# S4 convolution and LSTM-like scan on one core: the input and Toeplitz operands of groups 1 to 15 as pairs of f16 parts

## The reference, cut to what matters

```
def _L0_attn_ref(r, ...):                       # r: (8, 2048, 512), batch b, time l, channel h
    K = _dplr_kernel(Bc, Cc, Pc, Qc, Lam, step_c, seq_len)          # (512, 2048)
    Kf = jnp.fft.rfft(K, n=nfft, axis=-1)
    uf = jnp.fft.rfft(r, n=nfft, axis=1)
    h1 = jnp.fft.irfft(uf * Kf.T[None], n=nfft, axis=1)[:, :seq_len]
    y1 = h1 + D[0] * r
    return jax.nn.gelu(y1, approximate=False)
...
x = L0_attn_r
x = x + _layernorm(_L0_attn_ref(_layernorm(x, axis=-1), ...), axis=-1)
x = x + _layernorm(_L0_ffn_ref(_layernorm(x, axis=-1), ...), axis=-1)
```

## Time and profile before

| what | value |
|---|---|
| median of 3 runs | 2649.8 us (2649.52 to 2650.55) |
| the profiled execution | 2650.23 us, its span 2648.6 us |
| TensorE busy | 2526.6 us, 95% of the span |
| VectorE, ScalarE, GpSimd busy | 1841.0, 1623.0, 1133.2 us (70%, 61%, 43%) |
| the convolution, 137 to 581 us | TensorE busy 440.07 of 444 us |
| chain of waits, by engine | TensorE 84%, VectorE 4%, GpSimd 4%, ScalarE 3%, DMA 3% |

### The profile page before, as it was taken

One profiled execution on the slowest core, in us unless ns is written; L12 is line 12 of the kernel. 1 busy time (PEld: TensorE's weight loads), 2 busy tenths in 40 slices (PEclk: granted clock), 3 DMA queues, 4 the chain that ended last, 5 costly groups with the idle time before them and its releaser, 6 DMA issues.

```text
span 2648.6 us, 57574 instructions
## 1 busy us (share of the span) xinstructions
PE 2526.6 (95%) x22659; PEld 2205.2 (83%) x22659; DVE 1841.0 (70%) x3413; ACT 1623.0 (61%) x3003; POOL 1133.2 (43%) x1437
## 2 busy tenths in 40 slices
PE   5499999997899999999999999999999999999997
PEld 4278888886788888888888888888888888888886
DVE  7855556558887677766777887776677764467666
ACT  8656667567665555555556665555555553378777
POOL 7768686725332223222234332322223220068667
PEclk9799999998999999999999999999999999999999
DMA  8779797889674556445655755544555432489998
GB/s 355 286 227 312 267 314 270 271 293 343 181 196 116 130 139 167 119 116 131 141 167 150 204 152 143 166 116 116 135 137 168 119 82 49 168 333 362 370 359 321
DMA packets 507551, 542.52 MB, mean 205 GB/s; under 512 B 273936, under 2 KB 412944, under 8 KB 488720
## 3 DMA queue, kind: packets, MB, share of 16 engines
q1 hardware_dynamic: 507280, 538.85, 65.3%
HBM read 292.88 MB, written 180.88 MB: 179 GB/s over the span
## 4 chain that ended last, share of the span: by engine, by line
PE 84%; DVE 4%; POOL 4%; ACT 3%; DMA 3%; issue 2%; SPq 1%; DVEq 0%; POOLq 0%; ACTq 0%
PE bank L2138 31%; PE bank L2148 29%; PE bank L2194 8%; PE bank L2027 4%; PE bank L1977 3%; PE bank L2013 3%; PE bank L2035 2%; PE bank L1989 2%; PE bank L2169 2%; DVE big L1827 1%; PE bank L1997 1%; ACT big L1343 1%; POOL big L886 1%; POOL big L990 1%; DVE big L1884 1%
## 5 line engine op out<-in xcount | busy, mean ns | idle before, releaser
L2138 PE MATMUL bank<-big 128*128 128x256 f16 x8064 | 1078.8, 273 | 20.8 <-ACT big L1387 8.3
L2148 PE MATMUL bank<-big 128*128 128x256 f16 x7056 | 962.5, 273 | 0.0
L2138 PEld LDWEIGHTS bank<-big 128*128 128x128 f16 x8064 | 790.4, 98 | 117.4 <-ACT big L1387 9.9
L2148 PEld LDWEIGHTS bank<-big 128*128 128x128 f16 x7056 | 690.4, 98 | 79.9
L1031 POOL TENSOR_SCALAR big<-big 128x1 f32<-128x1 f32 x253 | 108.0, 427 | 1084.8 <-DVE big L1674 806.4
L1884 DVE TENSOR_TENSOR big<-bank,big 128x512 f32<-128x512 f32 x256 | 175.1, 684 | 197.1 <-PE bank L2148 195.0
L2194 PE MATMUL bank<-big 128*128 128x256 f16 x2688 | 295.3, 273 | 4.4 <-ACT bank L1323 4.0
L1299 ACT ACTIVATE big<-big 128x512 f32<-128x512 f32 x384 | 289.6, 803 | 13.5 <-DVE big L1884 13.4
L2194 PEld LDWEIGHTS bank<-big 128*128 128x128 f16 x2688 | 262.4, 98 | 37.0 <-ACT bank L1323 4.9
L1870 DVE TENSOR_TENSOR big<-bank,big 128x512 f32<-128x512 f32 x256 | 176.3, 689 | 140.9 <-PE bank L2148 118.5
L1231 ACT ACTIVATE big<-big 128x512 f32<-128x512 f32 x256 | 205.9, 808 | 100.3 <-POOL big L1033 96.5
(11 more groups left out here) (233 smaller groups left out, 3724.3 us busy)
## 6 DMA issues: line engine op xcount, KB each, us to landing
xtd<-big SPq DMA_DIRECT2D x60, 1024.0 KB, 7.0
big<-xr SPq DMA_DIRECT2D x16, 2048.0 KB, 8.7
big<-xg SPq DMA_DIRECT2D x64, 512.0 KB, 7.8
big<-kpad SPq DMA_DIRECT2D x32, 1024.0 KB, 12.2
yd<-big SPq DMA_DIRECT2D x16, 2048.0 KB, 16.8
big<-x SPq DMA_DIRECT2D x128, 256.0 KB, 3.1
x1d<-big SPq DMA_DIRECT2D x128, 256.0 KB, 3.1
big<-x1d SPq DMA_DIRECT2D x64, 512.0 KB, 8.5
```

Of the source, the lines that this page charges most:

```text
L2138: ins = e.matmul(o, WX[2 * g + lw][:, q, kt, 128 * a:128 * a + 128], slot[u % 2][:, part, lx, k0 + kt, :], start=(first and kt == 0 and (l ...
L2148: ins = e.matmul(o, WC[2 * g + lw][:, q, kt, 128 * a:128 * a + 128], cc[unit(u)[1] % 2][:, qc, lx, kt, :], start=False, stop=end, skip_gro ...
```

## The change

For groups 1 to 15 the products of `conv_input`, and of `state_in` for chunks 4 to 15, become three f16 products each. Group 0, and chunks 0 to 3 of every group in `state_in`, stay in f32.

- `kpad` holds 32-bit words, each the f16 high part and the f16 low part of one kernel value. They are made once in the setup, by one ScalarE and two GpSimd instructions. The Toeplitz matrix of one part is then a view of `T` in which each f16 weight stands 4 bytes from the next (`T16[...][:, h, :, lw]`).
- The input of group g lands and is normalized in f32 in one staging buffer `us` of one group. ScalarE copies a chunk to f16 (`input_high`, 128x256), VectorE subtracts (`input_low`, 128x256), both into `u16[g % 2]`. Steps 0 to 3 of iteration g cut two chunks each, steps 4 to 11 one each (`SPLIT_AT`): 16 instructions on each of the two engines per group, 240 in all.
- A quarter of group g+1 can be loaded only when its place in `us` has been cut: the loads move to steps 4, 4, 8 and 12 of iteration g and wait for `ulo`. GpSimd normalizes the quarters in the order 1, 0, 2, 3, after its four subtractions for weights.
- `Gm` is cut into `Gm16` by two GpSimd instructions. `load_WX` of i = 15 moves to step 12. The store of `kpad` moves from k = 10 to k = 11 of the setup.

The core of the diff:

```
+NORM_ORDER = NORM_FIRST + [4 * g + q for g in range(2, NG) for q in (1, 0, 2, 3)]
+SPLIT_AT = [(4, 0), (5, 1), (6, 2), (7, 3)] + [(k,) for k in range(8, 16)] + [()] * 4
...
+def split_count(g, k):
+
+    return 16 * (g - 1) + SPLIT_ORDER.index(k) + 1
...
             def load_u(n):
                 g, q = divmod(n, 4)
-                if g >= 3:
-                    w.wait_ge(s["cv"], G * (g - 2))
+                if g >= 2:
+                    w.wait_ge(s["ulo"], split_count(g - 1, 4 * q + 3))
+                    if q == 0:
+                        w.wait_ge(s["st"], 14 * (g - 1) + 3)
...
-                for q in range(4):
-                    load_u(4 * (i + 1) + q)
...
                 for j in range(16):
+                    if i < NG - 1:
+                        for q in {4: (1, 0), 8: (2,), 12: (3,)}.get(j, ()):
+                            load_u(4 * (i + 1) + q)
+                    if i == NG - 1 and j == 12:
+                        w.wait_ge(s["ulo"], 16 * (NG - 1))
+                        w.wait_ge(s["st"], 14 * (NG - 1) + 3)
+                        w.wait_ge(s["wd"], stored(6))
+                        for n in range(4):
+                            load_WX(n)
...
+            def input_high(g, k):
+                w.wait_ge(s["nrm"], norm_place(4 * g + k // 4) + 1)
+                if g >= 2:
+                    w.wait_ge(s["cv"], G * (g - 1))
+                e.activation(u16[g % 2][:, 0, k], us[:, k // 4, k % 4], ACT.Copy).then_inc(s["uhi"], 1)
...
+            def input_low(g, k):
+                w.wait_ge(s["uhi"], split_count(g, k))
+                e.tensor_tensor(u16[g % 2][:, 1, k], us[:, k // 4, k % 4], u16[g % 2][:, 0, k], SUB).then_inc(s["ulo"], 1)
...
+                w.wait_ge(s["Gh"], 2)
+                w.wait_ge(s["ulo"], split_count(g, k))
+                for a, (lw, lx) in enumerate(PARTS):
+                    e.matmul(o, Gm16[lw], u16[g % 2][:, lx, k].rearrange("p h b -> p (h b)"), start=(a == 0), stop=False)
...
-                e.matmul(o, T[t % 3][:, h % 16, :], u[g % 3][:, :, h, :], start=(q == 0), stop=False, skip_group_check=True)
+                if g == 0:
+                    e.matmul(o, T[t % 3][:, h % 16, :], u32[:, :, h, :], start=(q == 0), stop=False, skip_group_check=True)
+                    return
+                for a, (lw, lx) in enumerate(PARTS):
+                    e.matmul(o, T16[t % 3][:, h % 16, :, lw], u16[g % 2][:, lx, :, h, :], start=(q == 0 and a == 0), stop=False, skip_group_check=True)
```

More of the change, by code:

```diff
@@ L92, in norm_place @@
 def norm_place(n):
-    return NORM_FIRST.index(n) if n < 8 else n - 1
+    return NORM_ORDER.index(n)
+def split_count(g, k):
+    return 16 * (g - 1) + SPLIT_ORDER.index(k) + 1
 def pieces(g):
@@ L352, in s4_lstm_program @@
         t0_at = top[0]
-        T[0], u[0] = turns16(), rows()
+        T[0] = turns16()
+        u0_at = top[0]
+        u[0] = rows()
         x0_at = top[0]
@@ L360, in s4_lstm_program @@
         conv0 = top[0]
-        T[1], T[2], u[2] = turns16(), turns16(), rows()
+        T[1], T[2] = turns16(), turns16()
+        u2_at = top[0]
+        u[2] = rows()
         x1_at = top[0]
@@ L364, in s4_lstm_program @@
         y0_at = top[0]
+        u32 = u[0]
+        us = u[1].rearrange("p (q k) h b -> p q k h b", q=4)
+        u16 = [big[:, a:a + 4096].bitcast(F16).rearrange("p (l k h b) -> p l k h b", l=2, k=16, h=G) for a in (u0_at, u2_at)]
+        T16 = [t.rearrange("p h t -> p (h t)").bitcast(F16).rearrange("p (h t l) -> p h t l", h=16, l=2) for t in T]
         Y = [take(4096).rearrange("p (b k h) -> p b k h", b=8, k=16) for _ in range(2)]
@@ L370, in s4_lstm_program @@
         scl = take(16).rearrange("p (r n) -> p r n", r=2)
+        stts_at = top[0]
         stts = take(32).rearrange("p (n s) -> p n s", s=8)
@@ L1019, in pool_program @@
             for i in range(1, NG - 1):
-                for q in range(4):
-                    if i % 4 >= 2 and q == 0:
-                        quarter_sums(i)
+                if i % 4 >= 2:
+                    quarter_sums(i)
+                for q in (1, 0, 2, 3):
                     norm(4 * (i + 1) + q)
@@ L1204, in act_program @@
                         outm(i, j)
+                    if i < NG:
+                        for k in SPLIT_AT[j]:
+                            input_high(i, k)
                     for step, n, f in WEIGHTS_AT[i, j]:
@@ L1613, in dve_program @@
                         outm(i, j)
+                    if i < NG:
+                        for k in SPLIT_AT[j]:
+                            input_low(i, k)
                     for step, n, f in WEIGHTS_AT[i, j]:
@@ L1967, in state_in @@
                     w.wait_ge(s["nrmc"], k - 11)
-                else:
+                elif g == 0 or k < 4:
                     wait_u(4 * g + k // 4)
@@ L2021, in conv_input @@
                 w.wait_ge(s[f"T{t % 3}"], 16 * (t // 3 + 1))
-                for piece in range(4 * g, 4 * g + 4):
-                    wait_u(piece)
+                if g:
+                    w.wait_ge(s["ulo"], 16 * g)
+                else:
+                    for piece in range(4):
+                        wait_u(piece)
                 if q == 0 and n >= NC:
                     w.wait_ge(s["gl"], n - NC + 1)
-                e.matmul(o, T[t % 3][:, h % 16, :], u[g % 3][:, :, h, :], start=(q == 0), stop=False, skip_group_check=True)
+                if g == 0:
+                    e.matmul(o, T[t % 3][:, h % 16, :], u32[:, :, h, :], start=(q == 0), stop=False, skip_group_check=True)
+                    return
+                for a, (lw, lx) in enumerate(PARTS):
+                    e.matmul(o, T16[t % 3][:, h % 16, :, lw], u16[g % 2][:, lx, :, h, :], start=(q == 0 and a == 0), stop=False, skip_group_check=True)
             def conv_state(g, h):
```

53 lines of the change are left out of this document (31 added, 22 removed).

## The result

| | before | after |
|---|---|---|
| median of 4 runs each, us | 2649.74 | 2730.54 (2728.23 to 2733.24) |
| ratio, 95% interval | | 1.0304 (1.0292 to 1.0316) |
| profiled execution: time, span, us | 2650.2, 2648.6 | 2732.5, 2730.7 |

The change makes the kernel 81 us slower; the prediction had said 15 us faster. The place is plain from the positions of TensorE's step 5 (the start of its outm piece in each iteration). The 14 iterations from step 5 of i = 1 to step 5 of i = 15 take 414.25 us before and 490.79 after: +76.5 of the span's +82.1. Step 5 of i = 1 comes 3.6 us later, iterations 15 and 16 are 3.4 shorter, from the last conv_state to the first product of the next stage 24.1 us pass instead of 18.3, and the rest is 0.4 shorter. Every iteration became slower: 4, 8 and 12 take 33.5 to 34.9 us instead of 28.9, the others 33.3 to 38.3 instead of 29.3 to 31.6.

The account below looks back on a forecast made before the run. TensorE's own work was taken as the bound between 137 and 581 us. Gross gain 41.1 us less losses of 6.8, 12.6, 3.0, 1.0, 2.0 and 1.0 gave -14.7: 2635 us, range 2610 to 2668.

Parts of the forecast that it names:

- VectorE's subtraction: Input split in the convolution: 240 subtractions on VectorE, 0.42 us each like the state's instruction, 0.35 packed, 84 us in all.
- a rule on TensorE's pace: Skill's 81 ns per f16 load-and-product pair: conv_input 0.49 us for 0.45, convolution part losing 9 us instead of gaining 24.6.
- full steps: Rival for the convolution's steps: ScalarE and VectorE eat the whole gain, copies at 0.38, 2650 us, no change; chance 0.08.
- TensorE's gross gain: Convolution: conv_input 0.34 us for 0.45 (24.6 us), state_in 0.33 for 0.43 (16.5 us), 41.1 us together; iteration 16 not counted.
- Rival 1, strided weights: conv_input: f16 weights 4 bytes apart load at the f32 passes' pace, 0.75 us for 0.45, about 2705 us; chance 0.12.
- Rival 2, the ring: Staging buffer: loads taking 10 us make quarter 0 2.4 us late in 13 iterations, +31, 2666 us; chance 0.13.
- Steps 0 to 3, and ScalarE's copy at 0.30: Each iteration's start: two 0.30 us copies before the next state, two steps in 3.35 to 3.40 us, 6.8 us lost.
- Iterations with weights: Steps 5 to 14: ScalarE packed by seven copies, stretch stays at 18.5 us; 1.8 lost in 7 iterations, 12.6 us.
- TensorE's wait for the state copy: Convolution: TensorE's waits for ScalarE's state copy were to rise from 8.9 us to some 20 us, as a sign.
- iterations without weights: Convolution iterations in which no weights are made: 27.0 to 27.5 us each, against 29.3 before.
- The end: End of the convolution: load_WX moves close to the output's load, costing 1.0 us, bounds 0 to 4.
- The setup: Setup: small added instructions on GpSimd and ScalarE cost nothing, or 2 us if their cover is gone.

Follow-up runs that it names:

- e4: The changed kernel with the subtraction's second operand taken from a zeroed PSUM bank (low part wrong) and two gelu banks instead of three: 2655.97 us.
- e5: The changed kernel with normalization (groups 2 to 15), ScalarE's copy and VectorE's subtraction (groups 3 to 15) cut to one column, work left out: 2636.74 us.
- e3: The changed kernel with each GpSimd normalization instruction cut into four of 256 columns, nothing left out: 2678.93 us.
- e7: The changed kernel with ScalarE copying each f32 input chunk to PSUM and VectorE making both parts from there, two gelu banks: 2731.97 us.
- e8: As e7, but two chunks at once, with the quarters' loads moved and load_WX behind the output's load: 2707.42 us.
- e10: As e8, but ScalarE makes the high part and copies it to PSUM, and VectorE only subtracts: 2712.15 us.

## Why the prediction was wrong

By its own steps:

- **VectorE's subtraction: the step that failed.** "VectorE's 240 subtractions I take at the state's 0.42, 0.35 packed." The state's instruction reads PSUM and SBUF, the subtraction reads SBUF twice, and only the subtraction waits for GpSimd. Shape and type were matched with the nearest row, where the operands lie was not. Measured 0.92 on average, and each long one stands between a piece and the next state. Cost: 74.6 us (after less e4). The profile of the kernel before already had it. Its group of the same kind takes 0.70 us in the stage of products:

```profile
L1698 DVE TENSOR_TENSOR big<-big 128x512 f16<-128x512 f32 x248 | 168.0, 702 | 15.6 <-ACT big L1258 14.8
```

  And in the setup one of the same form meets GpSimd's normalization. VectorE, then GpSimd:

```profile
86.21 2.73 DVE L1531 TENSOR_TENSOR big<-big 128x512 f16<-128x512 f32 x1
89.41 1.82 DVE L1533 TENSOR_SCALAR big<-big 128x128 f32<-128x128 f32 x1 [0.48 <-DVE big L1531]
```

```profile
85.85 2.53 POOL L972 TENSOR_TENSOR big<-big 128x1024 f32<-128x1024 f32 x1
88.46 2.69 POOL L974 TENSOR_TENSOR big<-big 128x1024 f32<-128x1024 f32 x1
```

  2.73 us for an instruction of 0.70, beginning inside GpSimd's first and ending 0.56 after it, as the accumulations of e4 do. From it, and from GpSimd's 310 busy us of 444, a price could have been set: GpSimd is busy 0.70 of the time, a subtraction that meets it waits about half of its 2.39, so 0.4 + 0.70 x 1.2 = some 1.2 us as an estimate, against 0.92 measured (only 125 of the 240 met it). Times 240 that is about 200 us more than I had taken: VectorE's 255 + 84 would have become some 540 of 444 us, and VectorE the bound. The Trainium skill states this rule (SBUF — State Buffer, SBUF: two separate sides, on the pair of ports that VectorE and GpSimd share): whichever starts first holds the pair for its whole instruction and the other fully blocks; on VectorE's side this goes for instructions in a two-port mode, and for those with two SBUF inputs against a GpSimd instruction that reads SBUF. The traces agree on two inputs in SBUF: 0.40 to 0.43 us with one operand in PSUM, up to 2.60 with none. L1533 above (1.82 us) and L1692 in e4, each with one input and both held, would be the two-port mode; that they run in it no view here shows. I weighed a rule on TensorE's pace and not this one, and no rival named it: the slower rivals were weights, loads and full steps.
- **TensorE's gross gain: the price right, the sum too high.** Blocks cost what was forecast. TensorE in order of time, one step of iteration 5:

```profile
303.67 0.28 PE L2054 MATMUL bank<-big 128*128 128x256 f16 x1 [0.55 <-DVE big L1585]
303.79 0.49 PE L2036 MATMUL bank<-big 128*128 128x256 f16 x3
304.11 0.48 PE L2098 MATMUL bank<-big 128*128 128x120 f16 x6
```

  state_in takes 0.32 us from start to start (forecast 0.33); conv_input, six products from 351.77 to 352.11 in iteration 7, takes 0.34. But even e5, where split and normalization cost next to nothing, has only 31.4 us less busy time in the 14 iterations and 11.3 more idle, net 20.1. With 3.9 more in iterations 15 and 16 that makes 24.0 us, where 41.1 were counted, 43.7 with iteration 16. Which waits fill the 15.1 idle us was not taken apart further.
- **Rival 1, strided weights: false.** 0.34 for six products is 57 ns each, as the forecast had worked out from conv_state. The 81 ns of the Trainium skill (TensorE: Matmul & The Clock Gate, Back-to-back issue gap) would have made 0.49; the trace doesn't agree at 128 columns either.
- **Rival 2, the ring: false.** Loads of the staging buffer land in 4.2 us, median of 56, where they took 7.7; the Toeplitz loads in 8.2 instead of 12.2. In e4, where TensorE is as fast as before, it is 5.3 and 9.0. GpSimd waits for loads, but TensorE waits for GpSimd only the 2.1 us that it waited before.
- **Steps 0 to 3, and ScalarE's copy at 0.30: right.** In e4 the states of steps 1 and 3 stand 3.32 us apart (475.54 to 478.86, iteration 12), forecast 3.35 to 3.40; two copies take 0.62 (417.18 to 417.80).
- **Iterations with weights: right in kind.** In e4 the states of step 5 to step 14 span 18.75 us (453.45 to 472.20, iteration 11), forecast 18.5, and the whole iteration 29.2, forecast 28.7. TensorE's wait for the state copy, forecast at some 20 us, is 32.0 in e4; the 18.6 in the changed kernel is near the forecast by luck, as the subtraction takes most of the waits there. Of the iterations without weights, forecast at 27.0 to 27.5, only 4, 8 and 12 take 27.4 to 27.5 in e4; 13 takes 28.3, and 1, 5 and 9 take 32.1 to 34.6.
- **Work that the prediction left alone.** The weighted sum of weights (L1641 before, L1692 and L1694 in e4), now in the way of the normalization: some 7 us in e4, nothing forecast. That GpSimd's work changes its place in the iteration was read only for the ring.
- **The end: too low.** 1.0 forecast, 5.8 measured, and 5.0 and 5.6 in e4 and e5. VectorE waits 12.3 us for the output's load after, 9.0 before, and that load takes 11.1 and 11.7 us in e4 and e5 instead of 8.6; the rest of it stays open. The setup, forecast at nothing, is 3.6 us late after and 0.6 to 4.7 in the other runs, which stays open too.

The sum with what was measured: +74.6 for the exclusion, and e4's own +6.2 against before. In e4's trace these are 1.3 at the start, 2.8 in the 14 iterations (where TensorE's gain is eaten by full steps and by the weighted sum), 3.4 less in iterations 15 and 16, 5.0 at the end and 0.6 behind it.

## What to carry to other kernels

When a new VectorE instruction is priced from a row, match where its operands lie as well as its shape: with one in PSUM it costs 0.41 us here whatever GpSimd does, with both in SBUF 0.40 to 2.60: it ends 0.28 us after the GpSimd instruction that it met. Before adding such an instruction, and before moving GpSimd's work to another place, lay the two engines side by side in order of time; the unit of the price is the length of GpSimd's instruction, so short GpSimd instructions (e3: 52 us back) or an operand in PSUM (e4: 75 us back) are the two remedies, and the second is one only if the operand is in PSUM anyway (e7, e8 and e10 put it there, and are no faster than e3). A split into f16 parts that saves TensorE 0.1 us a block is worth less than that figure times the blocks: 24 of 44 us in the convolution here, with all else nearly free.

## What was not expected of the hardware

- A VectorE instruction with both operands in SBUF that begins inside a GpSimd instruction here never ends before it: all 125 subtractions of that kind end 0.28 to 0.31 us after it. Even one column costs 0.58 us on average beside GpSimd, 0.19 without.
- An f32 tensor_scalar of 128x512 with its one operand in SBUF is held in the same way (0.48 us free, 1.20 to 2.45 in e4), a reduction of the same operand size is not (0.68 us either way).
- Six f16 pairs of load and product of 128 columns pass in 0.34 us with weights 4 bytes apart, 57 ns each; packed ones of 120 columns take 53.
- Cutting GpSimd's instruction of 1024 columns (2.4 us) into four of 256 (0.81 each) makes GpSimd slower, and still made the kernel 52 us faster.
